# A delta-rule stage with three key and query buffers, the next call's projection spread over the whole call, and tree seating in three steps a batch

## The reference, cut to what matters

```
q, k, v = (silu(causal_conv4(x @ W)) for W in (Wq, Wk, Wv))      # q and k of unit length
retained = einsum('bhvk,bhk->bhv', state, k_t)
state = a_t * (state - b_t * outer(retained, k_t)) + b_t * outer(v_t, k_t)
o_t = einsum('bhvk,bhk->bhv', state, q_t)
out = (rms_normalised(o) * o_norm_w * silu(x @ Wg)) @ Wo
```

## Time and profile before

| | before |
|---|---|
| median of 3 runs | 4735.28 us (4730.35 to 4737.99) |
| profiled execution | 4733.8 us, its span 4731.9 us |
| mean granted TensorE clock | 0.881 |
| PE busy | 3756.7 us (79%) |
| DVE busy | 2299.2 us (49%) |
| ACT busy | 1536.4 us (32%) |
| POOL busy | 783.7 us (17%) |

### The profile page before, as it was taken

One profiled execution on the slowest core, in us unless ns is written; L12 is line 12 of the kernel. 1 busy time (PEld: TensorE's weight loads), 2 busy tenths in 40 slices (PEclk: granted clock), 3 DMA queues, 4 the chain that ended last, 5 costly groups with the idle time before them and its releaser, 6 DMA issues. The chain is left out here.

```text
span 4731.9 us, 63721 instructions
## 1 busy us (share of the span) xinstructions
PE 3756.7 (79%) x23891; PEld 2900.5 (61%) x23900; DVE 2299.2 (49%) x4786; ACT 1536.4 (32%) x3511; POOL 783.7 (17%) x756
## 2 busy tenths in 40 slices
PE   4688998789998869999843777831665999999998
PEld 4477877668777758778742665621553555555544
DVE  5455566445556625565531443460343344444444
ACT  1444444334434424444411222200212333333331
POOL 0010101421011150101122222014231011111110
PEclk8899998889989979989966888965877899999999
DMA  4100000310000040000016785325753000000000
GB/s 154 58 17 12 20 6 10 111 50 19 15 19 6 15 151 15 19 15 6 5 67 200 252 264 187 116 76 177 229 208 135 14 19 19 23 23 23 19 14 14
DMA packets 229966, 331.60 MB, mean 70 GB/s; under 512 B 34209, under 2 KB 154529, under 8 KB 229281
## 3 DMA queue, kind: packets, MB, share of 16 engines
q1 hardware_dynamic: 187936, 235.10, 15.5%
q0 software_dynamic: 22528, 67.26, 3.9%
q10 hardware_dynamic: 19200, 25.17, 1.4%
HBM read 225.50 MB, written 101.97 MB: 69 GB/s over the span
## 5 line engine op out<-in xcount | busy, mean ns | idle before, releaser
L724 PE MATMUL banks<-s_d_X,s_d_M 128*128 128x128 f32 (+1 forms) x3072 | 441.2, 293 | 52.6 <-DVE s_d_X L785 51.4
L724 PEld LDWEIGHTS banks<-s_d_X,s_d_M 128*128 128x128 f32 x3072 | 417.3, 209 | 81.9 <-DVE s_d_X L785 56.8
L785 DVE COPY_PREDICATED s_d_X<-c_mask,banks 128x512 f32<-128x512 uint32 x320 | 232.7, 733 | 390.5 <-PE banks L740 385.2
L764 ACT ACTIVATE s_d_W<-banks 128x512 f32<-128x512 f32 (+1 forms) x384 | 216.2, 563 | 634.5 <-PE banks L724 608.7
L740 PE MATMUL banks<-s_d_W,s_d_Pf 128*128 128x128 f32 x2560 | 326.5, 280 | 20.3 <-ACT s_d_Pf L767 14.2
L507 PE MATMUL banks<-s_d_xT,s_w_qkvg 128*128 128x512 f32 x640 | 311.8, 611 | 37.8 <-DMA s_d_xT<-xnT 18.2
L740 PEld LDWEIGHTS banks<-s_d_W,s_d_Pf 128*128 128x128 f32 x2560 | 310.8, 194 | 45.4 <-issue 30.6
L2206 ACT ACTIVATE s_g_pT<-banks 128x1536 f32<-128x1536 f32 (+1 forms) x96 | 152.9, 1592 | 451.7 <-PE banks L2094 451.7
L596 DVE SCALAR_TENSOR_TENSOR s_d_kq<-banks,s_conv_w,s_d_kq 128x511 f32<-128x511 f32 (+2 forms) x384 | 285.6, 744 | 12.1 <-ACT s_d_kq L552 3.0
L2170 DVE TENSOR_REDUCE s_g_nmax<-banks 128x4 f32<-128x512 f32 (+3 forms) x128 | 188.0, 1490 | 192.5 <-PE banks L2078 192.4
L1357 PE MATMUL banks<-c_ident,s_q_xs 128*128 128x128 f32 x256 | 44.5, 317 | 251.7 <-DMA s_q_xs<-xs 243.3
(11 more groups left out here) (351 smaller groups left out, 7642.6 us busy)
## 6 DMA issues: line engine op xcount, KB each, us to landing
s_q_w<-w12p SPq DMA_DIRECT2D x252, 257.0 KB
s_q_xs<-xs SPq DMA_DIRECT2D x32, 516.0 KB, 5.3
s_q_acc<-xs SPq DMA_DIRECT2D x32, 512.0 KB
s_r_xT<-xfT SPq DMA_DIRECT2D x12, 1024.0 KB
s_r_work<-xf SPq DMA_DIRECT2D x24, 512.0 KB
og<-s_d_o SPq DMA_DIRECT2D x16, 512.0 KB
s_b_og<-og SPq DMA_DIRECT2D x8, 1024.0 KB, 9.3
s_x_in<-x SPq DMA_DIRECT2D x8, 512.0 KB, 4.4
```

The costliest lines, as they stand in the source:

```text
L724: ins = e.matmul(a[:, h * P:h * P + nW], self.M[p][:, h, :], self.X[p][:, h, 0:nW], start=True, stop=True)
L764: e.activation(self.W[p][:, :, 0:nW], bk[2 * p][:].rearrange("p (h n) -> p h n", h=H)[:, :, 0:nW], ACT.Copy).then_inc(self.W_made, 1)
L785: e.copy_predicated(self.X[p][:], g.mask[:, l, 1, None, :].broadcast_to((P, H, P)), a[:].rearrange("p (h n) -> p h n", h=H)).then_inc(self ...
```

## The change

Keys and queries get a third buffer, chosen by the call's number modulo 3; the room for it comes from E, which now shares W's memory, and from the routes' work buffer, whose comparisons move into `xT` of the routes. Waits that guarded the two buffers together are placed where each is needed: o_gated ahead of the gate's silu, stepped ahead of the values' copy, and for the keys and queries the state of three calls ago. The decay rates are loaded 16 projection steps later. In `walk` the six setup steps of a pair are treated apart from the 18 others: the projection runs from the first step of a call to its last (4, 18, 8 and 20 steps), the old call's second state over the whole first pair (3 and 15 steps), this call's first state over the 18 later steps of the second pair, and the routes only beside the 18 steps, at 0.82 each. A batch of the seating takes three steps in place of one, a tree 155 in place of 137.

```diff
@@ class Delta, __init__
-        self.kd, self.kq, self.sgw = two("kinds", [P, KINDS, TPB, H]), two("kq", [P, H, 2, SEQ]), two("gate", [P, TPB, 256])
+        self.kd, self.sgw = two("kinds", [P, KINDS, TPB, H]), two("gate", [P, TPB, 256])
+        self.kq = [sb(f"d_kq{j}", [P, H, 2, SEQ]) for j in range(3)]
...
-        self.E, self.M, self.X, self.W = (two(n, [P, H, P]) for n in ("E", "M", "X", "W"))
+        self.M, self.X, self.W = (two(n, [P, H, P]) for n in ("M", "X", "W"))
+        self.E = self.W
...
-    def dest(self, par, n, h):
-        return self.vT[:, h, :] if n == "v" else self.kq[par][:, h, 0 if n == "k" else 1, :]
+    def dest(self, n, what, h):
+        return self.vT[:, h, :] if what == "v" else self.kq[n % 3][:, h, 0 if what == "k" else 1, :]
@@ project_sync
-            if u == self.ITEM + 8:
+            if u == self.GATE + 4:
                 if n >= 2:
                     e.wait_ge(self.stepped, 28 * (n - 1))
                 e.dma_start(self.kd[par][:]...
@@ project_scalar
-                if j == 0 and n >= 2:
-                    e.wait_ge(self.o_gated, n - 1)
+                if j == 0 and n >= 3:
+                    e.wait_ge(self.stepped, 28 * (n - 2))
...
             if q is not None:
+                if q == 0 and n >= 2:
+                    e.wait_ge(self.o_gated, n - 1)
...
             if r is not None:
+                if r == 0 and n >= 2:
+                    e.wait_ge(self.stepped, 28 * (n - 1))
@@ walk
-        routes = (beside, 0.56)
         finish(project(e, 0))
         last = iter(())
         for n in range(self.CALLS):
             ahead = project(e, n + 1) if n + 1 < self.CALLS else iter(())
-            next(ahead, None)
-            main = invert(e, n, 0)
-            side_by_side((next(main, None) for _ in range(12)), (last, 1.5), routes)
+            main, here = invert(e, n, 0), state(e, n, 0)
+            side_by_side((next(main) for _ in range(6)), (last, 0.5), (ahead, 0.67))
+            side_by_side(main, (last, 0.84), (ahead, 1.0), (beside, 0.82))
             finish(last)
-            side_by_side(main, (ahead, 1.4), routes)
-            side_by_side(invert(e, n, 1), (state(e, n, 0), 0.55), (ahead, 1.4), routes)
-            finish(ahead)
+            main = invert(e, n, 1)
+            side_by_side((next(main) for _ in range(6)), (ahead, 1.34))
+            side_by_side(main, (here, 0.67), (ahead, 1.12), (beside, 0.82))
+            finish(here, ahead)
             last = state(e, n, 1)
@@ class Routes
-    LEAD, RANKING, SEATING = 8, 28, N_BATCH + 1
+    LEAD, RANKING, SEATING = 8, 28, 3 * (N_BATCH + 1)
...
-        self.work = sb("work", [P, 3 * RT * LEAVES])
+        self.work = sb("work", [P, 2 * RT * LEAVES + RT * P])
@@ steps_sync (a new tree's loads)
                 e.wait_ge(self.routed, self.V * 4 * F)
+                e.wait_ge(self.sorting, self.SORT * F)
@@ sort_vector
-        cmp = self.work[:, 2 * TPB * ROW:]
+        cmp = self.xT[:].rearrange("p c n -> p (c n)")
@@ steps_sync, steps_vector, steps_gpsimd: behind each of the batches
-                yield
-            yield
+                for _ in range(3):
+                    yield
+            for _ in range(3):
+                yield
```

More of the change, by code:

```diff
@@ L494, in project_tensor @@
         g, bk, par = self.g, self.g.bank, n % 2
-        xT, w, vT, kq = self.xT, self.w, self.vT, self.kq[par]
+        xT, w, vT, kq = self.xT, self.w, self.vT, self.kq[n % 3]
         for u in range(self.STEPS):
@@ L548, in project_scalar @@
                     e.wait_ge(self.v_turned, 2 * n)
-                if j == 0 and n >= 2:
-                    e.wait_ge(self.o_gated, n - 1)
+                if j == 0 and n >= 3:
+                    e.wait_ge(self.stepped, 28 * (n - 2))
                 e.wait_ge(self.projected, 10 * n + j + 1)
-                e.activation(self.dest(par, what, h), bk[6 + j % 2][:], ACT.Copy, scale=cw[:, par, k0 + 3:k0 + 4]).then_inc(self.tap0, 1)
+                e.activation(self.dest(n, what, h), bk[6 + j % 2][:], ACT.Copy, scale=cw[:, par, k0 + 3:k0 + 4]).then_inc(self.tap0, 1)
             if i is not None and i % 2 == 0:
                 for k in (i, i + 1):
-                    d = self.dest(par, *self.ITEMS[k])
+                    d = self.dest(n, *self.ITEMS[k])
                     e.wait_ge(self.tap, 3 * (10 * n + k + 1))
@@ L589, in project_vector @@
                 what, h = self.ITEMS[j]
-                k0, d = self.TAP[what] + 4 * h, self.dest(par, what, h)
+                k0, d = self.TAP[what] + 4 * h, self.dest(n, what, h)
                 for a in (1, 2, 3):
@@ L628, in setup_tensor @@
         g, bk, par, m, p = self.g, self.g.bank, n % 2, 2 * n + t // 2, t % 2
-        kd, kq, low, high = self.kd[par], self.kq[par], bk[2 * p], bk[2 * p + 1]
+        kd, kq, low, high = self.kd[par], self.kq[n % 3], bk[2 * p], bk[2 * p + 1]
         if m:
@@ L805, in state_tensor @@
         bk, par = self.g.bank, n % 2
-        kq, S = self.kq[par], self.S
+        kq, S = self.kq[n % 3], self.S
         for t in (2 * pair, 2 * pair + 1):
```

## The result

The changed kernel takes 4445.96 us (median of four runs, 4440.28 to 4451.94) beside 4732.82 us (four runs, 4717.11 to 4737.99) for the kernel before on the same chip: a ratio of 0.9405, 95% interval 0.938 to 0.9429. The forecast was 4496 us in a range of 4390 to 4630. All lines of the code lie 3 to 15 lower down than before: L516 is now L519, L824 L831, L740 L747, L724 L731, L785 L792, L596 L603; the gathers L1249 are L1263 and the scatters L1256 L1270.

The account below looks back on a forecast made before the run. PE, busy 79% of the span, was taken as the bound, through its waits in the delta walk; -73 - 38 - 68 - 60 = -239 from 4733.8 gave 4494.8, or 4496 us against the median, range 4390 to 4630.

Parts of the forecast that it names:

- the two terms of the calls: In the walk's ordinary calls: shorter PE waits in the pair setups, -68 us, and less time at low clock, -60 us.
- The clock, -60: Ordinary calls: half of the 8.5 us a call that the low PE clock costs returns, 4.3 x 14 calls, -60 us.
- The setup waits, -68: Both pairs' setups: spread projection and earlier taps cut PE waits from 10.7 to 6.2 us a call, 15 calls, -68 us.
- The seating, -73: Two calls seating trees: slower batches remove their 103 us excess, less 15 us of waiting kept for each, -73 us.
- The tail, -38: After the walk's last state: only four gathers and five scatters remain, 55 us of POOL instead of 92, -38 us.
- Costed at nothing: Extra table loads (20.5 us of ACT), E in W's memory, xT comparisons, later decay rates: no time added.
- DVE as the bound: First half of a call: DVE about 80% busy, gives back the -68 and -60, total 4623 us; chance 0.20.
- A late gate: Second tile's setup: first gate matmul waits for item 9's taps, delaying tile and gates; with 10 us late, 4795; chance 0.07.
- Slow seating: Seating batches: each of eight DMAs waits for a DVE tap instruction, 5 us a batch over two trees, 4586 us; chance 0.06.
- the first rival: First half of a call: DVE becomes the bound at about 80% busy, total 4623 us; chance 0.20.
- the second's: Seating in the walk: indirect DMAs slowed by the port shared with DVE, total 4586 us; chance 0.06.

## Why the prediction was right, point by point

**The direction and the place** were right: no call of 180 us (the longest is 141.6), ordinary calls near 125 (121.8), a tail near 55 us (63.8), L519's wait about halved (69.1 to 37.8), the clock above 0.95 in the walk (0.98 from 193.5 to 2060.4 us). The time came out 50 us below the forecast, inside the range, and that owes something to luck: the two terms of the calls (-68 and -60) were 52 us too small together, the seating's 18 too large, and 15 us came from the first call and the stages outside, which I had not priced.

**The clock, -60**, was mis-sized. I took half of what the low clock cost, 4.3 us a call; PE's busy time fell by 6.0 us a call, at 0.99 nearly all there was. So the 8.5 us that I worked out for the whole was too much, and the half that I took of it too little. The waits of 0.8 to 2.5 us that stand in the place of the earlier trace rows are seldom followed by a stretch like the 24 us at 0.51 in the earlier trace rows.

**The setup waits, -68**, came out larger, for a reason that the forecast only half named. What is left was worked out as 6.2 us a call and is 6.0; what was there I took from one call, 10.7, and the mean was 12.8. The gate's 2.7 us and the masked copy's 0.8 show as 2.45 and 1.66 above. But I put the gain down to the projection that fills the setups and to earlier taps. Taking the projection out of both setups gives back 4.3 us of the 12.85 a call; putting the state back to its old pace and place gives back 11.8, and with it there the projection over the whole call does nothing. The state's new pace and place clear the setups, and I had no term for them. The order of the links in the first setup was read rightly, the term that moves them was not.

**The seating, -73**, was mis-sized on the other side: 48 us remain in three calls, not 30 in two, and the last call lost the 13 us that the others gained, as half a seating lies in it. My 15 us a seating stood for lateness; DVE's wait for late scatters was not it, since that is gone and a slower pace left as much. What is left goes with the gathers: without them it is zero, and with most runs split into fours it is halved. No row of before had been read for that, beside DVE's 52.5 us of waiting in the earlier trace rows.

**The tail, -38**, measured 41; of POOL's own part, 92 us, 51 are left where 55 were worked out.

**Costed at nothing**, and rightly: the third buffer and E in W's memory (0.9995). The table loads came as expected, 14 more in the walk's silus (45 instead of 31, 1283 ns each), 18 us of ACT; they were not tried by themselves.

**The rivals.** DVE as the bound: at 67% in ordinary calls it is not, and L731's waits for L792 are 18.0 us in the whole walk. A late gate: its wait for DVE's taps is gone. Slow seating by the port that VectorE and GpSimd share (its price took 5 us a batch where its own sum gives 6): gathers of successive batches begin at 1516.84, 1528.88, 1541.03 and 1553.09, the 12.1 us of the earlier trace rows, with DVE busy 52% of that call instead of 40%. By the rule of the Trainium skill (SBUF — State Buffer, "SBUF: two separate sides") that pitch could have grown; this trace does not show it. The section ties the lock to VectorE operations in a two-port mode, or with two SBUF inputs against a GpSimd operation that reads SBUF, a condition that I had left out, so this is no full test of it. The trace shows the other engines late instead, and ACT among them, of which the same section says that it never waits on anyone; so the rule does not explain that either.

**Two slips in the range.** The 4623 that had to be held is the first rival's, not the second's, and two thirds of every term's reach give 4372 to 4609, not 4390 to 4600. The result lies inside either way.

## What to carry to other kernels

A chain of short hand-overs between engines should be dealt out over the longest stretch of other work there is, before anything is moved in to fill the gaps: the filler was worth 4.3 us a call once the chain was spread, and spreading the filler brought nothing while the chain stood in the setups. Short waits also cost what comes behind them: here PE's waits fell by 6.8 us a call, and its busy time by 6.0 as the clock rose. And pace work on a side engine by what it does to the others, not only by whether it keeps up.

## What was not expected of the hardware

While POOL issues eight indirect DMAs in one run (9.9 us), DVE and ACT began 3.0 and 4.3 us after the matmuls whose results they read, in the batch shown, with nothing in the profile behind the wait. PE's idle time is 1.86 us in a run of eight, and 0.04, 0.24 and 0.58 in runs of four of three kernels; a run of four is half as long (4.8 us). What carries it stays open. That the gathers' own small transfers have a part in it is not excluded: without them the excess is zero, with split runs it is only halved, and no run kept eight DMAs while it took the gathers' transfers away.
